# State space on one core: the gate product leaves VectorE, with a ScalarE copy out of PSUM and the product on GpSimd

## The reference

```
xn = rmsnorm(layernorm(x)) * norm_w
xi, res = split(xn @ in_proj_w)                 # 2 x 256 channels
xi = silu(causal_conv4(xi) + conv_b)
delta, Bm, Cm = split(xi @ x_proj_w)            # 64, 16, 16
delta = softplus(delta @ dt_proj_w + dt_proj_b)
state_t = exp(delta_t * A) * state_(t-1) + delta_t * B_t * xi_t    # 256 channels x 16 states
y_t = sum over the 16 states of state_t * C_t
y = (y + xi * D) * silu(res)                    # the gate product
out = y @ out_proj_w + x
```

## Time and profile before

| | |
|---|---|
| median of 3 runs | 1350.16 us (1346.49 to 1353.12) |
| profiled execution: time | 1351.29 us |
| profiled execution: span from first to last instruction | 1349.5 us |
| mean granted TensorE clock over the span | 0.900 |
| state space block with its scan (chunks 0 to 7) | about 545 to 1027 us of the span |
| gate products, first and last start | 615.1 and 1022.5 us (8) |

### The profile page before, as it was taken

The page is one execution under the profiler, slowest core; times in us unless marked ns, Lnnn a source line. Parts: engine busy times, 40 slices in busy tenths (PEclk is TensorE's granted clock), DMA queues, the critical chain, the costliest instruction groups (busy, mean ns, idle before and its releaser), DMA issues. The chain is left out here.

```text
span 1349.5 us, 20293 instructions
## 1 busy us (share of the span) xinstructions
PE 1057.1 (78%) x4202; PEld 615.6 (46%) x4203; DVE 945.9 (70%) x2283; ACT 746.9 (55%) x1826; POOL 834.6 (62%) x602
## 2 busy tenths in 40 slices
PE   3888867449999955888989888897784229999995
PEld 3666745327777831333333333333223215555563
DVE  4999899633333333799999999989997715455573
ACT  3767746235555547858586776756531115555542
POOL 1433248447517557877886888788782577437276
PEclk9999879569999976999999999899898559999998
DMA  8994002226524425343434354443540026435335
GB/s 244 160 148 138 1 8 24 18 35 88 81 57 88 85 33 111 86 143 131 156 115 169 124 157 124 135 160 115 184 143 0 32 57 94 83 74 95 79 67 103
DMA packets 140460, 133.22 MB, mean 99 GB/s; under 512 B 14579, under 2 KB 121699, under 8 KB 140259
## 3 DMA queue, kind: packets, MB, share of 16 engines
q1 hardware_dynamic: 107106, 115.55, 32.2%
q0 software_dynamic: 33280, 16.86, 11.2%
HBM read 98.66 MB, written 31.60 MB: 97 GB/s over the span
## 5 line engine op out<-in xcount | busy, mean ns | idle before, releaser
L1740 POOL TENSOR_TENSOR ss_HC<-ss_Hs,ss_Cb 128x512 f32<-128x512 f32 x256 | 317.6, 1270 | 91.7 <-PE ss_Y L1514 70.7
L1514 PE MATMUL ss_Y<-ss_HC,g_ident 128*128 128x512 f32 x512 | 267.8, 641 | 46.4 <-POOL ss_HC L1740 38.8
L1809 DVE TENSOR_TENSOR_SCAN ss_Hs<-ss_dA,ss_dBu 128x512 f32<-128x512 f32 x256 | 297.2, 1203 | 6.3 <-ACT ss_dA L1656 6.0
L827 POOL DMA_INDIRECT rows<-m_XS,g_slot x128 | 181.3, 1417 | 69.2 <-issue 35.8
L1127 PE MATMUL m_x_UP<-g_m_w,m_x_gT 128*128 (+1 forms) x532 | 204.5, 491 | 6.7 <-issue 2.6
L1656 ACT ACTIVATE ss_dA<-ss_delta,g_A 128x510 f32<-128x510 f32 x256 | 167.7, 712 | 56.9 <-DVE ss_Hs L1809 56.7
L1514 PEld LDWEIGHTS ss_Y<-ss_HC,g_ident 128*128 128x128 f32 x512 | 90.2, 197 | 207.1 <-POOL ss_HC L1740 148.1
L1801 DVE TENSOR_TENSOR ss_dBu<-ss_duP,ss_Bb 128x512 f32<-128x512 f32 x256 | 163.4, 685 | 21.0 <-DMA ss_Bb<-bc_rows 16.7
L1147 PEld LDWEIGHTS m_x_DP<-g_m_w,m_x_hT 128*128 128x128 f32 (+1 forms) x908 | 131.5, 190 | 80.0 <-issue 38.3
L1147 PE MATMUL m_x_DP<-g_m_w,m_x_hT 128*128 (+3 forms) x908 | 161.7, 296 | 5.3 <-ACT m_x_hT L1214 3.1
L1107 POOL DMA_INDIRECT g_X<-out_rows,g_slot x64 | 99.3, 1551 | 80.1 <-DMA out_rows<-m_x_YO 57.5
(11 more groups left out here) (266 smaller groups left out, 1826.5 us busy)
## 6 DMA issues: line engine op xcount, KB each, us to landing
ss_Bb<-bc_rows SPq DMA_DIRECT2D x64, 512.0 KB, 4.9
ss_Cb<-bc_rows SPq DMA_DIRECT2D x64, 512.0 KB, 4.0
rows<-g_Z SPq DMA_DIRECT2D x2, 5031.0 KB, 55.3
m_x_G<-rows SPq DMA_DIRECT2D x156, 64.5 KB
out_rows<-m_x_YO SPq DMA_DIRECT2D x156, 64.0 KB
g_m_w<-in_w_up SPq DMA_DIRECT2D x1, 2816.0 KB, 10.2
g_m_b<-in_b SPq DMA_DIRECT2D x1, 2160.0 KB, 11.5
g_X<-in_x SPq DMA_DIRECT2D x4, 512.0 KB, 5.7
```

Of the source, the lines that this page charges most:

```text
L827: self.nc.gpsimd.indirect_dma_start(self.XG, bass.IndirectOffsetOnAxis(self.rt.slot[k][:, t:t + 1], 0), self.XS[:, t, :], None, compute_op ...
L1514: ins = nc.tensor.matmul(Yp[:, h, :], ident[:], HC[n % 2][:, h, :], start=False, stop=n == N - 1)
L1740: nc.gpsimd.tensor_tensor(HC[n % 2][:, h, :], Hs[n % 4][:, h, :], Cb[g % 2][:, n % 2, :], ALU.mult).then_inc(hc_ready.sem, 1)
L1809: v_.tensor_tensor_scan(Hs[n % 4][:, h, :], dA[n % NA][:, h, :, :].rearrange("p s t -> p (s t)"), dBu[:, h, :], 0.0, ALU.mult, ALU.add).th ...
```

## The change

`Yp` is read by ScalarE instead of VectorE: a new step `copy_y(c - 1)` copies it into a new SBUF tile `yc`, and its signal `y_copied` frees `Yp` for `w_D`. GpSimd then makes the product of `yc` and the gate from SBUF (`gate_rows`, moved), and signals `gated`. In ScalarE's order the copy stands at n = 2 behind the powers and ahead of `log_dt`; in GpSimd's order the product stands behind HC(2). After the last chunk both stand at the end of the engines' programs. VectorE's product is gone.

```
-        yg = m.sb("yg", [P, 2, CH])
+        yc, yg = m.sb("yc", [P, 2, CH]), m.sb("yg", [P, 2, CH])
...
                 def accumulate(n, c, v):
                     if n == 0:
                         if at(c, 0, 1):
-                            pe.wait_ge(gated.sem, gated.after(c - 1))
+                            pe.wait_ge(y_copied.sem, y_copied.after(c - 1))
...
+                def copy_y(c):
+                    act.wait_ge(summed.sem, summed.after(c))
+                    if at(c, 0, 1):
+                        act.wait_ge(gated.sem, gated.after(c - 1))
+                    nc.scalar.activation(yc[:], Yp[:], ACT.Copy).then_inc(y_copied.sem, 1)
...
-                        if n == 2 and back:
-                            log_dt(c + 1)
+                        if n == 2:
+                            if at(c, 0, 1):
+                                copy_y(c - 1)
+                            if back:
+                                log_dt(c + 1)
...
                 chunks(act, scan)
+                copy_y(NCH - 1)
...
+                def gate_rows(c, v):
+
+                    pool.wait_ge(gate_ready.sem, gate_ready.after(c))
+                    pool.wait_ge(y_copied.sem, y_copied.after(c))
+                    if at(c, 0, 1):
+                        pool.wait_ge(out_ready.sem, out_ready.after(c - 1))
+                    nc.gpsimd.tensor_tensor(yg[:], yc[:], gate[v][:], ALU.mult).then_inc(gated.sem, 1)
...
+                        if n == 2 and at(c, 0, 1):
+                            gate_rows(c - 1, 1 - v)
                         if back and 3 <= n < 7:
                             softplus_step(pool, nc.gpsimd, n - 3, c + 1, 1 - v)
 
                 chunks(pool, scan)
+                gate_rows(NCH - 1, 1)
...
-                def gate_rows(c, v):
-
-                    dve.wait_ge(gate_ready.sem, gate_ready.after(c))
-                    dve.wait_ge(summed.sem, summed.after(c))
-                    v_.tensor_tensor(yg[:], Yp[:], gate[v][:], ALU.mult).then_inc(gated.sem, 1)
...
-                        if n == 2 and at(c, 0, 1):
-                            gate_rows(c - 1, 1 - v)
...
                 chunks(dve, scan)
-                gate_rows(NCH - 1, 1)
                 update(NCH - 1)
```

More of the change, by code:

```diff
@@ L1378, in state_space @@
         hc_ready, summed = m.sig("hc_ready", 2 * N), m.sig("summed", N)
-        gated, out_ready, x_updated = m.sig("gated"), m.sig("out_ready"), m.sig("x_updated")
+        y_copied, gated, out_ready, x_updated = m.sig("y_copied"), m.sig("gated"), m.sig("out_ready"), m.sig("x_updated")
         def seqs(a):
```

## The result

The changed kernel takes 1390.28 us (median of 4 runs, 1388.86 to 1393.87); the kernel before took 1351.43 us beside it. The ratio is 1.0298 [1.0263, 1.0333]: 2.6 to 3.3% slower. The forecast was 1391. The profiled execution has 1389.54 us, a span of 1387.7 and a mean granted clock of 0.890.

What follows compares the result with a forecast made beforehand. A closed loop of GpSimd's products, TensorE's sums and ScalarE's copies was taken as the bound. 29.5 plus 10.8 for the clock, 40.3 on 1351.3, gave 1391.6, or 1391 us as median; 8-in-10 range 1373 to 1400.

Steps and rivals of the forecast that it cites:

- The copy's price and place: ScalarE's copy takes 1.02 us behind the powers of step 5; in chunk 3 `w_D` starts 3.97 us later.
- HC(3): On GpSimd in chunk 3, the late `w_D` and the product between HC(2) and HC(3) delay HC(3) by 5.33 us.
- rival "absorbed": GpSimd's 4.58 us of waits at HC(10) and HC(11) swallow the delay; 1357 us, chance 0.08.
- Update and output: Output matmul moves from 746.79 to about 748.3, `update` with it; both end before the late `Bb`, adding nothing.
- The clock: A new 3.9 us TensorE gap before `w_D` lowers the clock: 1.8 us in each of six chunks, +10.8 us.
- rival "no falls": The clock does not fall at `w_D`, leaving only the 29.5 us; 1380 us, chance 0.18.
- The end: At the section's end nothing covers copy 1.02, product 2.35 and handover 0.1, in place of 1.22: +2.3 us.
- Chunk 7 itself: `w_D` keeps its time; VectorE saves 1.14 us but waits 0.6 for `Bb`: -0.5 us.
- The sum: Chunks and end +29.5 us, clock +10.8: +40.3 us in all.
- The rival "faster": VectorE is the bound, as the page suggests, so dropping its gate product gains time; 1343 us, chance 0.05.

Runs made afterwards that it cites:

- e1: The changed kernel with ScalarE's copy moved ahead of the dt copies, GpSimd's product left behind HC(2); 1356.34 us, ratio 1.0032 to before.
- e4: The changed kernel with the copy still late but the product made by VectorE from `yc` at n = 4; 1383.56 us, ratio 1.0264 to before.
- e10: The changed kernel with only the residual update moved from behind scan(6) to behind scan(7) on VectorE; 1388.22 us, ratio 1.0287 to before.
- e5: The changed kernel with the gate matmuls of chunk c + 1 moved ahead of `w_D` on TensorE, copy still late; 1381.11 us, ratio 1.0248 to before.
- e2: The changed kernel with the copy ahead of the dt copies and GpSimd's product moved behind HC(1); 1352.37 us, ratio 1.0020 to before.
- e6: The kernel before with the third softplus step moved from GpSimd to VectorE at n = 7; 1343.15 us, ratio 0.9944 to before.
- e9: e7 with the last product on VectorE from PSUM and the residual update moved behind scan(7); 1338.22 us, ratio 0.9910 to before.
- e7: e2 with the third softplus step moved from GpSimd to VectorE at n = 7; 1344.14 us, ratio 0.9963 to before.
- e3: The changed kernel with only the copy moved, ahead of the powers of step 5, behind the dt copies; 1382.54 us, ratio 1.0241 to before.

## Why the prediction was right

The loop, not VectorE, sets the chunk, and every later row follows from it. By the steps of the prediction:

**The copy's price and place.** 1.02 taken, 1.03 measured. It was to start behind the powers of step 5, with `w_D` some 4 us late; TensorE's gap is 3.84. In chunk 1 `w_D` comes 86.29 us behind the first scan (613.68 - 527.39) and before it was 83.13: 3.16 later, 3.18 forecast (619.53 - 616.35). e1 shows that the place is what counts.

**HC(3).** `w_D` to HC(2) at the full clock plus 4.79 was the forecast; HC(2) to HC(3) is 4.75 (757.05 - 752.30). e4 gives the product's net share as 1.3 a chunk, where the difference of 5.33 and 3.97 is 1.36. The waits at HC(10) and HC(11) stayed within 0.02 of the earlier trace rows: the rival "absorbed" is out.

**Update and output.** Forecast to add nothing. The update does wait 2.68 us in chunk 3, which I had not seen, but by e10 the loop is the same without that wait. The idle time before the output matmul fell from 2.95 to 0.50, as forecast.

**The clock.** The term was 1.8 us in each of six chunks, 10.8. `w_D` to HC(2) takes 5.49, 6.50, 5.48, 6.51, 5.48 and 6.54 us in chunks 1 to 6 against 3.87: 12.8 in all, 2.1 a chunk. e5 isolates it with 13.5. So the fall came in every chunk, in three of them at 2.6, the upper end that I had kept. The rival "no falls" (1380) is near what e5 made: 1377.04 in the profiled execution, 1381.11 as median.

**The end.** Chunk 7 itself is as forecast: `w_D` to the last update grew by 2.85 (56.22 against 53.37), of which 3.50 are the end, so that -0.65 are left for the chunk, and -0.5 were forecast. The end was +2.3 by the forecast and is +3.5: the copy and the product cost what was said, but TensorE idles 3.58 us before the last output matmul, which then takes 3.28 instead of 2.05. I had left out that term.

**The sum.** Forecast +40.3 for the section; measured +43.5. The clock is 2.0 of the difference and the last output matmul 1.2. The whole time hit closer than that, 1390.28 against 1391, because the section began 5.8 us earlier in the profiled execution of after, in work that the change does not touch: 43.5 - 5.8 = 37.7 of the 38.2 by which the profiled executions differ. That part of the agreement is chance. Where the start of the section comes from is left open.

**The rival "faster".** The page's busy share spoke for VectorE. In the kernel before, taking work off VectorE is worth nothing (e2: 1.0020), taking a step off GpSimd is worth 7.8 us of the section although VectorE gets it (e6). Beyond this point VectorE is the bound, and only there could its gate product have a price: where the output matmul of e9 kept the full clock, the chunk is 57.7 us against 58.2 in e6. Of this e7 lost most to the wait for the output, and that e7 to e9 gain anything over e6 is not shown.

What the experiments do not separate: the shares of the loop's 37.5 us (product 7.8, clock 13.5, the rest of 16.1 the late `w_D` itself) come from kernels that each change one thing in after, and the 16.1 is only what is left over. Whether the two halves of the change add up can be read from e1 (late product, early copy) and e4 (late copy, no product on GpSimd): over the five intervals of chunks 1 to 6 they cost 4.1 and 28.5 us against before, 32.6 together, and the change 34.0. Over the whole loop it is 1.5 and 29.6 against 37.5; most of that gap is the interval to chunk 7, which the early copy shortens.

## What to carry to other kernels

Where the order on each engine is fixed, price a moved step by where it stands in the queue: the same copy and product cost 39 us of the whole behind the dt copies and the powers, and under 3 us in the wait that was there (e2). Before taking work off the busiest engine, look for its short regular waits; when they are there, it is another engine that must be relieved, and the gain ends as soon as the first one has no wait left. And a new gap on TensorE's path can be paid twice, once as time and once at the lower clock behind it; matmuls that are ready anyway, moved into the gap, gave the second part back here (e5).

## What was not expected of the hardware

The length of the idle time alone does not tell whether the clock falls. A gap of 2.62 us before `w_D` in e3 was followed by the lower level in all six chunks, 2.95 us before the output matmul in e7 too (3.59 us for the matmul), and the same 2.95 us of the earlier trace rows not (2.05 us). In e9 a gap of 3.04 us stood before the output matmul of chunks 2, 4, 5 and 6: it took 3.75 us in chunks 2 and 5 and 2.02 in chunks 4 and 6. What decides is left open.

A `tensor_tensor` of 128x1024 from SBUF took 1.20 to 2.26 us on VectorE in chunks 1 to 6 of e6 to e9. In the two chunks of e9 shown above the difference came with what GpSimd did beside it; on GpSimd a step of this shape took 2.35 in the earlier trace rows, beside VectorE operations that read one of their inputs from PSUM.
